# Decoder kernel on one core: one batch's norm and projection moved behind the first local tile, and the second local layer's first turn and product moved into the first layer's MLP

## The reference, cut to what matters

```python
x = _layernorm(x + self_attention(x))
x = _layernorm(x + cross_attention(x, ctx_1024))
x = _layernorm(x + ffn(x))

def _layer(x, wqkv, qs, ksc, wo, lg, lb, w1, b1, w2, b2):
    h = shift_token(x)
    qkv = h @ wqkv
    q, k, v = jnp.split(qkv, 3, axis=-1)
    ...
    q = l2norm(q) * qs
    k = l2norm(k) * ksc
    q, k = rotary_xpos(q, k)
    o = local_attention(q, k, v)
    x = x + o @ wo
    h = shift_token(x)
    h = (h - mu) / jnp.sqrt(var + 1e-05) * lg + lb
    h = h @ w1 + b1
    a, g = jnp.split(h, 2, axis=-1)
    h = a * jax.nn.gelu(g, approximate=False)
    x = x + h @ w2 + b2
for l in range(2):
    x = _layer(x, ...)
```

## Time and profile before

| | us |
|---|---|
| median of 3 runs | 2047.09 (2046.86 to 2048.8) |
| the profiled execution | 2047.91 |
| its span | 2046.1 |
| TensorE busy | 1953.4 (95%) |
| VectorE, ScalarE, GpSimd busy | 1650.6, 1525.4, 1249.7 |

### The profile page before, as it was taken

How to read it: one execution, slowest core, us unless ns; L and a number is a source line. 1 busy time by engine, 2 the same in 40 slices (tenths; PEclk the granted TensorE clock), 3 DMA queues, 4 the chain that set the end, 5 groups by cost and what they waited for, 6 DMA issues and landing times. The chain is left out here.

```text
span 2046.1 us, 55498 instructions
## 1 busy us (share of the span) xinstructions
PE 1953.4 (95%) x19773; PEld 1421.1 (69%) x19773; DVE 1650.6 (81%) x3927; ACT 1525.4 (75%) x3610; POOL 1249.7 (61%) x1184
## 2 busy tenths in 40 slices
PE   6999999999999999879999998999889999989997
PEld 5545555555555554458889887888678888888887
DVE  7888888988888889679999995664389999975775
ACT  2688888888888888738999887544289998884443
POOL 3445566544445443677888774554278877766775
PEclk9899999999999999989999999999899999999999
DMA  4233433333333334301000001100100000001211
GB/s 140 85 112 118 118 108 118 124 118 120 119 120 131 130 130 137 122 33 56 8 3 3 3 28 38 47 16 1 44 2 8 8 3 3 18 7 47 78 49 45
DMA packets 93639, 132.90 MB, mean 65 GB/s; under 512 B 13888, under 2 KB 45120, under 8 KB 93376
## 3 DMA queue, kind: packets, MB, share of 16 engines
q1 hardware_dynamic: 90816, 120.97, 18.3%
q0 software_dynamic: 2560, 8.39, 1.1%
HBM read 47.14 MB, written 29.89 MB: 38 GB/s over the span
## 5 line engine op out<-in xcount | busy, mean ns | idle before, releaser
L1248 DVE TENSOR_REDUCE MX<-PS 128x1 f32<-128x512 f32 x1024 | 641.3, 682 | 89.2 <-PE PS L718 85.7
L1059 ACT ACTIVATE PT<-PS 128x512 f32<-128x512 f32 x1024 | 553.6, 619 | 93.0 <-PE PS L731 90.1
L731 PE MATMUL PS<-QS,KS 64*128 64x512 f32 x1024 | 365.5, 436 | 3.3 <-ACT PT L1059 1.6
L718 PE MATMUL PS<-KS,QS 64*128 64x512 f32 x1024 | 353.0, 433 | 5.9 <-DMA KS<-HL 1.0
L731 PEld LDWEIGHTS PS<-QS,KS 64*128 64x128 f32 x1024 | 164.0, 185 | 245.4 <-issue 200.8
L747 PE MATMUL PS<-PT,VP 128*17 128x512 f32 x2048 | 269.5, 598 | 2.0 <-ACT OT L1066 1.2
L1629 POOL TENSOR_TENSOR PB<-PB,RC 128x512 f32<-128x512 f32 (+1 forms) x192 | 182.5, 959 | 135.9 <-DVE RC L1379 135.9
L1123 ACT ACTIVATE PB<-PB,NMf 128x256 f32<-128x256 f32 (+1 forms) x512 | 242.1, 491 | 0.0
L823 PE MATMUL PS<-WQ,XT 64*128 64x512 f32 x1536 | 218.0, 417 | 15.3 <-DVE RB L1333 8.9
L1369 DVE CUSTOM_DVE_ANT_0 PB<-PS,mk,RN 128x256 f32<-128x256 f32 (+1 forms) x512 | 203.8, 444 | 2.3 <-PE PS L894 1.9
L718 PEld LDWEIGHTS PS<-KS,QS 64*128 64x128 f32 x1024 | 168.2, 186 | 50.2 <-issue 38.8
(11 more groups left out here) (198 smaller groups left out, 4638.9 us busy)
## 6 DMA issues: line engine op xcount, KB each, us to landing
od<-OT SPq DMA_DIRECT2D x64, 256.0 KB, 2.7
QS<-HL SPq DMA_DIRECT2D x96, 128.0 KB
KS<-HL SPq DMA_DIRECT2D x96, 128.0 KB
QS<-HL SPq DMA_DIRECT2D x48, 256.0 KB
KS<-HL SPq DMA_DIRECT2D x48, 256.0 KB
OC<-od SPq DMA_DIRECT2D x32, 256.0 KB
OC<-rs SPq DMA_DIRECT2D x32, 256.0 KB
X<-x SPq DMA_DIRECT2D x8, 512.0 KB, 4.0
```

What stands on the lines that cost most here:

```text
L718: pe.matmul(PS[:, bank, :], QS[rows, s, h // 2, qt * P:(qt + 1) * P], KS[rows, s, h // 2, :], start=True, stop=True).then_inc(fills("amax" ...
L731: pe.matmul(PS[:, bank, :], KS[rows, s, pair, kt * P:(kt + 1) * P], QS[rows, s, pair, :], start=True, stop=True).then_inc(fills("score", v ...
L1059: act.activation(PT[:, kt % 2, 2 * i + half], PS[:, TURNS["score", vb, g, kt, half, i][0], :], ACT.Exp).then_inc(drains("score", vb, g, kt ...
L1248: dve.tensor_reduce(MX[:, vb % 2, h // 8, qt, c:c + 1], PS[:, TURNS["amax", vb, h, qt][0], :], AX, ALU.max).then_inc(drains("amax", vb, h, ...
```

## The change

It adds a table `LAST_PROJECTION` with the projection, residual, statistics, inverse root and norm of `vb` 14 at times in layer 0's tiles, and takes them out of `LAST_STEP`: projection, residual and statistics come at the end of step -3, behind the first tile's rotation and in front of the second tile's product; the inverse roots follow in step -2, the norm just in front of the first tile's `wadd` of the keys, the stores in step -1. The norm of `vb` 14 is done by VectorE (`norm_last`) instead of GpSimd, with a wait that keeps the count of `normed` in order. In `mlp_stages` of layer 0, the turn of batch 0 for layer 1 moves behind the last batch's `mup` 0, in banks 6 and 7, and tile 0's product, squares, sum and rotation move in front of the last batch's `mpart`. The warm-ups change in number (97 transposes in all before, 129 after), and one moves from the product of tile 3 of layer 1 to the transposes of its tile 0.

```diff
--- before.py
+++ after.py
@@ -88,10 +88,16 @@
     (49, "wtrh", (0, 0, 0)), (49, "wtrh", (0, 0, 1)), (49, "wtrl", (0, 0, 0)), (49, "wtrl", (0, 0, 1)),
     (50, "out_hi", (NV - 2, 0)), (50, "out_lo", (NV - 2, 0)), (52, "out_hi", (NV - 2, 1)), (52, "out_lo", (NV - 2, 1)),
     (54, "wqk", (0, 0, 0)), (54, "wqk", (0, 0, 1)),
-    (54, "proj", (NV - 2, 0)), (54, "res", (NV - 2, 0)), (54, "stats", (NV - 2, 0)), (54, "rstd", (NV - 2, 0)), (54, "norm", (NV - 2, 0)),
-    (55, "proj", (NV - 2, 1)), (55, "res", (NV - 2, 1)), (55, "stats", (NV - 2, 1)), (55, "rstd", (NV - 2, 1)), (55, "norm", (NV - 2, 1)),
 ) + tuple((35 + k if k < 4 else 41 + k, "split_qkv", (0, k)) for k in range(10)) + (
     (53, "ot_out", (NV - 1, 2)), (53, "collect", (NV - 1, 0)),
+)
+
+
+LAST_PROJECTION = (
+    (-2.03, "proj", (NV - 2, 0)), (-2.03, "res", (NV - 2, 0)), (-2.03, "stats", (NV - 2, 0)),
+    (-2.02, "proj", (NV - 2, 1)), (-2.02, "res", (NV - 2, 1)), (-2.02, "stats", (NV - 2, 1)),
+    (-1.72, "rstd", (NV - 2, 0)), (-1.71, "rstd", (NV - 2, 1)), (-1.31, "norm_last", (NV - 2, 0)), (-1.30, "norm_last", (NV - 2, 1)),
+    (-0.90, "norm", (NV - 2, 0)), (-0.39, "norm", (NV - 2, 1)),
 )
 
 
@@ -124,7 +130,7 @@
     first = {s[0] for s in FIRST_BATCH} | {"load_xt", "stack"}
     out += [(s[0], 0) + s[1:] for s in FIRST_BATCH] + [("split_w", 0, 2), ("split_w", 0, 3)]
     out += [("load_x", 2), ("load_bias",)]
-    last = {(kind,) + part for _, kind, part in LAST_STEP} | {(kind, NV - 1) + part for _, kind, part in LAST_BATCH} | set(LAST_HEADS)
+    last = {(kind,) + part for _, kind, part in LAST_STEP + LAST_PROJECTION} | {(kind, NV - 1) + part for _, kind, part in LAST_BATCH} | set(LAST_HEADS)
     places = {}
 
     def put(step, place, stage):
@@ -207,7 +213,7 @@
     held = []
     seam = [(when + NU, (kind, L) + part) for when, kind, part in MLP_FIRST]
     if L == 0:
-        seam += [(when, (kind, NV - 1) + part) for when, kind, part in LAST_BATCH] + [(3.0, ("load_mlp", 0))]
+        seam += [(when, (kind, NV - 1) + part) for when, kind, part in LAST_BATCH] + [(when, (kind,) + part) for when, kind, part in LAST_PROJECTION] + [(3.0, ("load_mlp", 0))]
     seam.sort(key=lambda s: s[0])
     first = min(k for _, _, k in WINDOW_ORDER)
     last = max(k + (BEHIND if kind == "wvo" else 0) for kind, _, k in WINDOW_ORDER)
@@ -266,7 +272,7 @@
     out = [("mout", L, 2), ("mshift", L, 2)]
     for n in range(NB + 2):
         if n == NB:
-            out += [("mpart", L, NB - 1, i) for i in range(4)]
+            out += (window_fill(1) if L == 0 else []) + [("mpart", L, NB - 1, i) for i in range(4)]
         for slot, kind, part, k in MLP_ORDER:
             b = n - k
             if b < 0 or b >= NB:
@@ -275,23 +281,23 @@
                 continue
             if not (kind == "mup" and b == 0 and part[0] < 5 or kind in ("mnorm", "mtr") and b == 1):
                 out.append((kind, L, b) + part)
-            if L == 0 and kind == "mtail" and b == NB - 1:
-                out += window_first(1) + window_fill(1)
+            if L == 0 and (kind, b) + part == ("mup", NB - 1, 0):
+                out += window_first(1)
             if kind == "mup" and slot % 2 and chores:
                 out += chores.pop(0)
     return out
 
 
 WARM = {
-    ("rope", 0, 0, 0): (7, 10),
-    ("val", 0, 0): (4, 18),
-    ("amax", 0, 1, 0): (6, 6),
-    ("wqk", 0, 1, 0): (2, 12),
-    ("wqkt", 0, 0, 0): (2, 13),
-    ("wqk", 0, 2, 0): (2, 6),
-    ("wqk", 1, 2, 0): (3, 13),
-    ("wqkt", 1, 1, 0): (3, 13),
-    ("wqk", 1, 3, 0): (3, 6),
+    ("rope", 0, 0, 0): (7, 18),
+    ("val", 0, 0): (4, 36),
+    ("amax", 0, 1, 0): (6, 9),
+    ("wqk", 0, 1, 0): (2, 15),
+    ("wqkt", 0, 0, 0): (2, 14),
+    ("wqk", 0, 2, 0): (2, 7),
+    ("wqkt", 1, 0, 0): (3, 12),
+    ("wqk", 1, 2, 0): (3, 8),
+    ("wqkt", 1, 1, 0): (3, 10),
 }
 
 
@@ -369,7 +375,7 @@
             turns[s] = (bank, n[bank], fills[bank])
         elif kind == "wtr":
             for half in range(2 if a[2] == 0 else 0):
-                use(("wtr",) + a[:2] + (half,), (6 if a[1] else 0) + half)
+                use(("wtr",) + a[:2] + (half,), (6 if a[0] or a[1] else 0) + half)
         elif kind == "wqk":
             for part in range(2 if a[2] == 0 else 0):
                 use(("wqk",) + a[:2] + (part,), part)
@@ -1280,12 +1286,14 @@
                 m.then_inc(sem["mean_var"], 1)
 
             def norm_last(vb, half):
-                b, T = NB - 1, LNT[:, half]
-                dve.wait_ge(sem["rstd"], 2 * NV - 1 + half)
+                b, T = vb % NB, LNT[:, half]
+                dve.wait_ge(sem["rstd"], 2 * vb + 1 + half)
+                if vb < NV - 1:
+                    dve.wait_ge(sem["normed"], 2 * vb + half)
                 for i in range(2):
                     x = X[:, b, 2 * half + i]
                     m = dve.tensor_scalar(x, x, T[:, 32 + 2 * i:33 + 2 * i], T[:, 48 + i:49 + i], ALU.subtract, ALU.mult)
-                m.then_inc(sem["normed_last"], 1)
+                m.then_inc(sem["normed" if vb < NV - 1 else "normed_last"], 1)
 
             def rotations(L):
                 dve.wait_ge(sem["rot_in"], 16 * (L + 1))
@@ -1567,7 +1575,7 @@
 
             def norm(vb, half):
                 b, T = vb % NB, LNT[:, half]
-                if vb < NV - 1:
+                if vb < NV - 2:
                     pool.wait_ge(sem["rstd"], 2 * vb + half + 1)
                     for i in range(2):
                         x = X[:, b, 2 * half + i]
```

## The result

| | before | after |
|---|---|---|
| median of 4 runs, us | 2047.41 (2046.86 to 2048.8) | 2033.18 (2030.13 to 2033.86) |
| the profiled execution, us | 2047.91 | 2033.19 |
| its span, us | 2046.1 | 2031.3 |
| mean granted clock | 0.981 | 0.986 |

The ratio is 0.9927, with a 95% interval of 0.9913 to 0.9942: faster, 14.2 us between the medians, 14.8 between the two spans. Forecast were 14.3 us and 2032.8. The sum is right, but the profile after shows that two of its three terms are not: the start gives 1.9 us instead of nothing, and the second seam some 2 us less than its 11.9.

A forecast was written before the change was run, and what follows sets the result against it. At two seams a chain through one pair of PSUM banks, not work, was taken as the bound. Gains 2.4 + 11.9 + 0 = 14.3 us gave 2032.8 us as the median, range 2026 to 2038.5.

The forecast's parts named there:

- the start: Before the kernel's first product: 8 more transposes inside a 3.28 us wait gain nothing; bounds nothing to 2.0 us.
- the second seam: First layer's MLP into second local layer: earlier turn of X and tile 0's product gain 11.9 us; bounds 9.3 to 13.0.
- The first seam: Attention into first local layer: moved batch 6 work starts `wqkt` of tile 0 at 881.6 instead of 884.01, gaining 2.4 us.
- The lower bound: First seam: if VectorE waited out a late inverse root, 1.3 us less, thus a gain of 1.1 us.
- No engine turns this batch before tile 24, so the later norm costs nothing else: First seam: batch 6's later norm has no further cost, as the batch is first turned at tile 24 of the layer.
- at the higher level it takes 3.3 instead of 4.3 us: Second seam: product behind `wqkt` of tile 0 runs at the higher clock level, making the gain 11.9 us at its end.
- products behind the 4 us wait over 5 us: Named sign of being wrong: products behind the 4 us wait take over 5 us.
- rival 2: Warm-ups don't hold the clock: second layer's `wqkt` and product run at the lower level, 2035.2 us; chance 0.15.
- lower bound of 9.3: Second seam: the gain left if tile 1's product takes 5.91 us instead of 3.3.
- the 10 transposes that end at 9.46 did not lift it: Kernel's start: reason for taking no gain there, as products behind those transposes start at the lower level.
- Rival 1: Clock kept more often: the start's 2.0 us and a faster product behind first seam's `wqkt`, 3.9 less, 2028.9; chance 0.27.
- Rivals 3 and 4: Shift is half or more absorbed further on, 2040 to 2046, chance 0.08; clock stays low, slower, 2053.6, chance 0.03.

The follow-up runs named there:

- e2: Kernel before with only the first seam's part: batch 6's stages moved, norm on VectorE, that seam's three warm-ups; 2043.69 us, ratio 0.998.
- e7: Kernel after with the reciprocal of the last batch's sums moved behind the first local tile's rotation in VectorE's queue; 2027.45 us, ratio 0.9907.
- e11: Kernel after with batch 6's norm left on GpSimd, at its new place, instead of VectorE; 2041.09 us, ratio 0.997.
- e3: Kernel before with only the second seam's part: changed `mlp_stages`, banks 6 and 7, the second layer's warm-ups; 2037.24 us, ratio 0.9942.
- e10: e7 with batch 6's residual, statistics, inverse roots and norm also put behind the second tile's rotation; 2031.76 us, ratio 0.9926.
- e4: Kernel after with all nine warm-up entries of the kernel before, in number and place; 2035.69 us, ratio 0.9933.
- e6: Kernel after with 30 instead of 12 identity transposes ahead of layer 1's first transposes; 2033.37 us, ratio 0.9933.
- e8: Kernel after with the reciprocal behind the first rotation and the 30 transposes of e6 together; 2028.54 us, ratio 0.9912.
- e9: e7 run once more, unchanged; 2029.88 us, ratio 0.9913.
- e5: Kernel after, unchanged, run again as yardstick of the second group; 2032.84 us, ratio 0.9936.

## Why the prediction was right, and where it was not

**The first seam, 2.4 us: right in mechanism, and in size at the place it was priced for.** Every step was met within 0.1 us once the start's 1.9 is taken off, and e2, with this part alone, gives 2.2 there. The limit named, the load of the sums in front of VectorE's queue, is shown by e7: taken away, it gives 3.1 us more. The lower bound, VectorE waiting for a late root, did not occur, but GpSimd ended 0.05 us ahead of VectorE. What the sum left out is that the gain need not stay at 2.4 further on: by tile 4 it was 2.9 us in the kernel after and 4.6 in e2, whose next tiles had the higher granted clock. "No engine turns this batch before tile 24, so the later norm costs nothing else" held with the norm on VectorE; at its new place on GpSimd the same norm costs 5.5 us more (e11).

**The second seam, 11.9 us: 9.5 measured.** The step that failed is "at the higher level it takes 3.3 instead of 4.3 us". The starts were right (9.6 and 10.9 us earlier in e3, forecast 9.8 and 10.9); the product took 5.73 and 5.81 us. That is one of the signs that the prediction itself named for being wrong (products behind the 4 us wait over 5 us). Behind 12 transposes and a wait for VectorE of 2.59 us the level was lost more often than not: besides the kernel after's 5.73, the six other profiles with this entry at 12 gave 5.81, 4.25, 3.41, 4.68, 3.40 and 5.80 us, the two with 30 gave 3.41 both. Where it was kept with 12 (e7 and e10), the seam was worth 12.5 us at tile 9 of layer 1, in the other five 8.9 to 10.2. I had the row that spoke against me, the fall of the level in the 4.04 us wait of the kernel before (mean granted clock 0.97 from 1468 to 1470 us, 0.50 from 1472 to 1474), and used it only for rival 2. The measured 9.5 lies at the lower bound of 9.3, which came from another place's 5.91 us.

**The start, nothing: 1.9 to 2.2 us measured.** The step that failed is "the 10 transposes that end at 9.46 did not lift it". That was true of the one trace at hand only. In three other profiles with 10 the level did rise: in e2 and e4 it rose among the transposes (2.04 and 2.14 us for ten instead of 2.34) and fell in the wait behind them, in e3 the first two products still ran at the higher level (0.47 and 0.39 us) and the fourth at the lower. With 10 it was never kept, with 18 it was kept in six of nine profiles. So the longer warm-up makes the gain likelier; it does not ensure it. Layer 0's first product, some 840 us on, came at 857.0 to 857.5 in those six, at 859.0 to 860.7 in the other three, and at 858.4 to 859.9 in the four with 10. The upper bound of 2.0 was the right size for a run that keeps the level.

So errors of +1.9 us (start), +0.5 (first seam, further on) and -2 to -2.4 (second seam) nearly cancelled; 14.3 came out as 14.2 by luck within a sum whose range was honest. One figure of that range does not come out of its own terms: rival 2 with the lower bounds of both seams (1.3 and 2.6 us less) is 2039.1, not 2038.5. Nothing hangs on it.

**The rivals.** Rival 1, the clock kept more often: its 2.0 us at the start came, its product in the first seam did not (4.67 us against 5.15, not 3.3), and tile 1's product there ran in 3.40 instead of 5.03 us without any gain at `wqkt`, since VectorE's work was waited for. Rival 2, the level lost behind `wqkt` of the second seam: its price came in full there (2.4 us). Its reason, that transposes don't hold the level, is not borne out: with 30 of them in the wait both profiles kept it. What the kernel after lacked may be that its 12 left TensorE standing still for 2.59 us; with two profiles that kept the level even so, this is argued and not shown. Rivals 3 and 4 did not come: the shift of 14.2 at 1473 is still 14.8 at the end.

**The Trainium skill.** The Trainium skill's page "TensorE: Matmul & The Clock Gate", Part 4 (PE-mode transpose), states that transposes don't count for the clock as matmuls do. By it no row of transposes would lift the level. In the kernel after TensorE did nothing but 8 transposes of X and then the 18 before its first product; the 18 took 2.79 us where 4.2 are needed at the lower level, and the first product took 0.47 us. For transposes of the identity as this kernel does them the measurements decide against the page.

## What to carry to other kernels

Price a moved step by who is queued behind it on each engine over the next two tiles, not only the first: on VectorE the norm's 1.6 us fitted in, on GpSimd the same norm cost 5.5 more, one to two tiles later, and e10 gave back a gain in the same way. Before moving work out of a chain's way, look for what stands ahead of the chain for a transfer's sake: one number, the reciprocal's place, was worth 3 us and gives the best kernel of this study. And price a product behind a wait like the one of 2.59 us here at both levels of the clock: the lower one came wholly or in part in five of seven profiles, and it is worth up to 2.4 us each time. A profile shows one execution, and so only one of the outcomes.

## What the runs showed of the hardware

- Identity transposes can raise TensorE's level: with only 8 other transposes ahead of them, 18 took 2.67 to 4.02 us in nine profiles, where the lower level would need 4.2 (18 x 0.234). 30 in a wait of 4.1 us left 0.62 us of it, and the product behind kept the higher level in both profiles (e6, e8).
- The level behind a wait differs between profiles of one program: the same product took 3.41 or 4.68 us (e7, e9) and 5.73 or 4.25 (after, e5). At the start, 18 transposes followed by a wait of 2.60 us kept the level in the kernel after and by 2.86 lost it in e8, but kept it at 2.88 and 2.91 in e5 and e9, and lost it at 2.36 in e11. The length of the wait alone doesn't decide; what does stays open.
- A level kept early can be lost later: in e6 and e8 the gain of 2.3 us behind `wqkt` came with two half products at 2.2 to 2.9 us further on. It need not be: in e7 and e10 the same two took 2.4 and 1.6 to 1.7 us.
